# Attention scores in three passes over 128 rows with the remainder in four row groups, and transposes by single query tiles

## What is computed

```python
scores = jnp.einsum('bhqd,bhkd->bhqk', q, k) * scaling
scores = scores + attn_bias[:, None, :, :]
attn = jax.nn.softmax(scores, axis=-1)
ctx = jnp.einsum('bhij,bhjd->bhid', attn, v)
x = _rmsnorm(x + ctx @ wo + bo, alpha1, gamma1)
ff = jax.nn.silu(x @ w1 + b1) @ w2 + b2
x = _rmsnorm(x + ff, alpha2, gamma2)
```

## Time and profile before

| | us |
|---|---|
| median of three executions | 1954.26 |
| lowest, highest | 1952.67, 1956.72 |
| the profiled execution | 1954.66 |
| its span in the profile | 1952.9 |
| attention phase (to the first L1356) | about 1031.8 of the span |
| one batch (one `xT` load to the next) | 475.03 to 537.73 |

### The profile page before, as it was taken

One profiled execution on the slowest core, in us unless ns is written; L12 is line 12 of the kernel. 1 busy time (PEld: TensorE's weight loads), 2 busy tenths in 40 slices (PEclk: granted clock), 3 DMA queues, 4 the chain that ended last, 5 costly groups with the idle time before them and its releaser, 6 DMA issues. The chain is left out here.

```text
span 1952.9 us, 35623 instructions
## 1 busy us (share of the span) xinstructions
PE 1923.0 (98%) x10336; PEld 1694.0 (87%) x10336; DVE 1326.7 (68%) x2315; ACT 1169.7 (60%) x1893; POOL 691.6 (35%) x806
## 2 busy tenths in 40 slices
PE   7999999999999999999999999999999999999998
PEld 5888888888888888888887999999999999999997
DVE  5777777777777777777887566566666655656654
ACT  4777777777877778777875444344444334444432
POOL 2000000000000000000246657666666766666653
PEclk9999999999999999999999999999999999999999
DMA  7555665556555665557744221122222112222001
GB/s 211 155 143 153 167 158 135 138 155 184 132 143 147 163 168 130 139 154 210 172 129 146 87 87 54 40 78 86 86 86 83 52 40 82 86 86 86 30 28 41
DMA packets 107796, 226.87 MB, mean 116 GB/s; under 512 B 15088, under 2 KB 43504, under 8 KB 105712
## 3 DMA queue, kind: packets, MB, share of 16 engines
q1 hardware_dynamic: 107760, 226.43, 40.2%
HBM read 108.93 MB, written 41.94 MB: 77 GB/s over the span
## 5 line engine op out<-in xcount | busy, mean ns | idle before, releaser
L772 DVE TENSOR_TENSOR pT_lo<-ps_t,pT_hi 128x1024 fp32r<-128x1024 f32 x256 | 313.4, 1224 | 139.7 <-ACT pT_hi L660 139.7
L660 ACT ACTIVATE pT_hi<-ps_t 128x1024 fp32r<-128x1024 f32 x256 | 262.7, 1026 | 179.6 <-PE ps_t L916 178.6
L562 POOL TENSOR_TENSOR in_lo<-rows,in_hi 128x512 fp32r<-128x512 f32 x48 | 63.7, 1329 | 858.8 <-ACT in_hi L639 858.8
L653 ACT ACTIVATE probs<-probs,neg_max 128x512 f32<-128x512 f32 x512 | 339.2, 713 | 2.4 <-DVE neg_max L764 2.3
L764 DVE CUSTOM_DVE_ANT_0 probs<-ps_s,adj_s 128x512 f32<-128x512 f32 x448 | 290.8, 687 | 40.9 <-PE ps_s L907 33.9
L1300 DVE TENSOR_TENSOR h_lo<-hidden,h_hi 128x512 fp32r<-128x512 f32 x192 | 168.8, 879 | 172.5 <-ACT h_hi L1237 172.4
L916 PEld LDWEIGHTS ps_t<-ident,probs 128*128 128x128 f32 x2048 | 239.9, 141 | 35.0 <-issue 0.4
L916 PE MATMUL ps_t<-ident,probs 128*128 128x128 f32 x2048 | 265.7, 272 | 0.2 <-DVE pT_lo L772 0.2
L1395 PE MATMUL ps_y<-w_hi,h_hi 128*128 128x384 f32 x768 | 257.9, 336 | 0.0
L1395 PE MATMUL ps_y<-w_hi,h_lo 128*128 128x384 f32 x768 | 256.8, 334 | 0.0
L1395 PE MATMUL ps_y<-w_lo,h_hi 128*128 128x384 f32 x768 | 256.8, 334 | 0.0
(11 more groups left out here) (111 smaller groups left out, 3749.9 us busy)
## 6 DMA issues: line engine op xcount, KB each, us to landing
q_both<-weights_lo SPq DMA_DIRECT2D x192, 192.0 KB, 3.9
ctx_dram<-ctx_stage SPq DMA_DIRECT2D x128, 224.0 KB
ctx_raw<-ctx_dram SPq DMA_DIRECT2D x16, 1792.0 KB, 7.2
k_hl<-weights_hi SPq DMA_DIRECT2D x192, 96.0 KB, 3.4
adj_first<-in_adj SPq DMA_DIRECT2D x32, 512.0 KB, 9.2
adj_s<-in_adj SPq DMA_DIRECT2D x32, 512.0 KB, 6.1
rows<-in_xT SPq DMA_DIRECT2D x16, 768.0 KB, 7.1
rows<-in_x SPq DMA_DIRECT2D x16, 768.0 KB, 6.1
```

The costliest lines, as they stand in the source:

```text
L653: nc.scalar.activation(probs[:, at, :], probs[:, at, :], ACT.Exp, scale=-1.0, bias=neg_max[:, at:at + 1]).then_inc(exp_done, 1)
L660: nc.scalar.activation(pT_hi[:, h % 2, 2 * pair:2 * pair + 2, :, :], ps_t[pair][:, :, :].rearrange("p q (k i) -> p q k i", k=TT), ACT.Copy)\
L772: nc.vector.tensor_tensor(pT_lo[:, h % 2, s, :, :].rearrange("p q k i -> p (q k i)"), ps_t[pair][:, :, :].rearrange("p q n -> p (q n)"), p ...
```

## The change

A head's scores now take three products, without low by low. The two operands `q_wide` and `k_wide` have 128 rows: q high, q high, the first 32 features of q low, against k high, k low, the first 32 features of k high. One matmul of 128 rows per query tile multiplies them. The last 16 features of q low by k high are a matmul of 16 rows; the four query tiles' ones lie at partitions 0, 32, 64 and 96 (four row groups of the array), each with its own copy of q's and k's rows. Group 1 is filled by a DMA (q) or is already there in `k_wide` (k); for the groups 0, 2 and 3 GpSimd makes six copies per head (`copy_tails`), of 16 x 512 for k and 16 x 128 for q, each behind a no-op, a k copy before the q copy of its group. The four score banks of a head are filled in one stretch at the even steps, one head ahead (`AHEAD` = 2): four matmuls of 128 rows, then the four of 16 rows. `ps_s` has four banks, `ps_t` two banks of one tile each. Transposes, pT_hi and pT_lo go by single tiles, and a tile's transposes wait for pT_lo of the tile before the last. The four logits of a head follow the two pT_lo of the even step on VectorE; v2 and v3 are ahead of the scores on TensorE. k2 moves from step 0 to 4, q0 from 6 to 7, the copies of x from steps 2, 3, 4 to 5, 5, 6, and the loads of the bias from 11 and 12 to 13. q's second high copy is gone. The stacking takes 11, 14 and 12 DMAs for the three tiles of q and 9, 11 and 9 for those of k, each of one part.

```diff
+TAIL = 32
+TAIL_ROWS = DH - TAIL
+GROUP = 32
+OWN = 1
+COPIED = (0, 2, 3)
+HIGH, LOW = 0, 1
+STACKS = {"q": [(HIGH, 0, 0, DH), (HIGH, DH, 0, DH), (LOW, 2 * DH, 0, TAIL), (LOW, None, TAIL, DH)],
+          "k": [(HIGH, 0, 0, DH), (LOW, DH, 0, DH), (HIGH, 2 * DH, 0, TAIL)]}
...
+def stacks_of(kind, t):
+    out = []
+    for h in heads_of_tile(t):
+        for part, row, first, past in STACKS[kind]:
+            for tile, src, dim, n in pieces_of_head(h, first, past):
+                if tile == t:
+                    out.append((h, part, None if row is None else row + dim - first, src, n))
+    return out
...
+def tail_heads(t):
+    return [h for h in range(H) if pieces_of_head(h, TAIL, DH)[0][0] == t]
...
-STACK_DMAS = [2 * len(heads_of_tile(t)) for t in range(KT)]
+STACK_DMAS = {kind: [len(stacks_of(kind, t)) for t in range(KT)] for kind in "qk"}
...
-AHEAD = 3
-SIDE = {0: ["k2"], 1: ["v0", "v1"], 2: ["v2", "v3"], 6: ["q0"], 8: ["k0"], 10: ["q1"], 12: ["k1"], 14: ["q2"]}
-XT_AT = (2, 3, 4)
+AHEAD = 2
+SIDE = {1: ["v0", "v1"], 2: ["v2", "v3"], 4: ["k2"], 7: ["q0"], 8: ["k0"], 10: ["q1"], 12: ["k1"], 14: ["q2"]}
+XT_AT = {5: (0, 1), 6: (2,)}
...
-PARTS_HI = {"q": (0, 2), "k": (0,)}
 WO_STEPS = ["q0", "k0", "q1", "k1"]
 W1_PARTS = 2
+W1_ORDER = (0, 3, 1, 2, 4, 5)
+W1_AT = {3: 2, 5: 3, 8: 4, 10: 5}
+SCALE_AT = {11: (0,), 13: (1,), 14: (2, 3)}
...
-        q_both = sb("q_both", [2 * DH, H, 2, N], FP32R)
-        k_hl = sb("k_hl", [2 * DH, H, N], FP32R)
+        wide_of = {"q": sb("q_wide", [WIDE, H, N], FP32R), "k": sb("k_wide", [WIDE, H, N], FP32R)}
+        tails = sb("tails", [P, H, N], FP32R)
+        q_tails = sb("q_tails", [P, H, P], FP32R)
...
-        ps_s = [pb(f"ps_s{i}", [P, N]) for i in range(2)]
-        ps_t = [pb(f"ps_t{i}", [P, 2, N]) for i in range(2)]
+        ps_s = [pb(f"ps_s{i}", [P, N]) for i in range(TT)]
+        ps_t = [pb(f"ps_t{i}", [P, N]) for i in range(2)]
...
+        x1T_banks = ps_s[0:KT]
...
-                sp.wait_ge(proj_hi, proj_hi_no(b, kind, t, len(PARTS_HI[kind])))
-                for h in heads_of_tile(t):
-                    for tile, src, dst, n in pieces_of_head(h):
-                        if tile != t:
-                            continue
-                        for part, row in enumerate((dst, DH + dst)):
-                            if kind == "q":
-                                to = q_both[row:row + n, h, :, :]
-                                part_of = stage[kind][src:src + n, part:part + 2, :]
-                            else:
-                                to, part_of = k_hl[row:row + n, h, :], stage[kind][src:src + n, part, :]
-                            sp.dma_start(to.bitcast(FP32), part_of.bitcast(FP32)).then_inc(stacked[kind][t], DMA)
+                sp.wait_ge(proj_hi, proj_no(b, kind, t))
+                for h, part, row, src, n in stacks_of(kind, t):
+                    to = tail(tails, OWN)[:, h, :] if row is None else wide_of[kind][row:row + n, h, :]
+                    sp.dma_start(to.bitcast(FP32), stage[kind][src:src + n, part, :].bitcast(FP32))\
+                        .then_inc(stacked[kind][t], DMA)
...
+                    for i in W1_ORDER[0:2]:
+                        load_w1(i)
+                if p in W1_AT:
+                    sp.wait_ge(w1_lo_done, W1_AT[p] - 1)
+                    load_w1(W1_ORDER[W1_AT[p]])
+                if p == 8:
...
-                    if p in (11, 12) and not last:
-                        load_adj_pair(b + 1, p - 11)
+                    if p == 13 and not last:
+                        load_adj_pair(b + 1, 0)
+                        load_adj_pair(b + 1, 1)
...
+            def copy_tails(b, h):
+                t = pieces_of_head(h, TAIL, DH)[0][0]
+                for kind in "qk":
+                    wait_apart(pool, stacked[kind][t], DMA * STACK_DMAS[kind][t] * (b + 1), consts_ready)
+                n = tails_no(b, h) - 2 * len(COPIED)
+                for g in COPIED:
+                    wait_past(pool, tails_copied, n)
+                    pool.nop(nofuse=True)
+                    pool.tensor_copy(tail(tails, g)[:, h, :], wide_of["k"][TAIL:DH, h, :]).then_inc(tails_copied, 1)
+                    pool.wait_ge(tails_copied, n + 1)
+                    pool.nop(nofuse=True)
+                    pool.tensor_copy(tail(q_tails, g)[:, h, :], tail(tails, OWN)[:, h, g * P:(g + 1) * P])\
+                        .then_inc(tails_copied, 1)
+                    n += 2
...
-                for p in XT_AT:
-                    xT_low(b + 1, p - XT_AT[0])
+                behind_tails(b, H - 1 - len(tail_heads(KT - 1)))
+                for ks in XT_AT.values():
+                    for k in ks:
+                        xT_low(b + 1, k)
+                pool.wait_ge(xT_split, KT * (b + 2))
+                for h in tail_heads(KT - 1):
+                    copy_tails(b, h)
+                for t in range(KT - 1):
+                    for h in tail_heads(t):
+                        copy_tails(b + 1, h)
...
+                pool.wait_ge(proj_ready, proj_no(LAST, "q", 2))
...
-                if kind == "q":
-                    act.wait_ge(proj_hi, proj_hi_no(b, kind, t, 1))
-                    nc.scalar.activation(stage[kind][:, 2, :], stage[kind][:, 0, :].bitcast(FP32), ACT.Copy)\
-                      .then_inc(proj_hi, 1)
...
-                wait_past(act, v_ready, TT * b)
+                wait_past(act, proj_ready, 2 * KT * b)
...
-            def pT_high(b, h, pair):
-                act.wait_ge(transposed, pair_no(b, h, pair))
+            def pT_high(b, h, qt):
+                act.wait_ge(transposed, score_no(b, h, qt))
                 wait_past(act, pv_ready, H * b + h - 1)
-                nc.scalar.activation(pT_hi[:, h % 2, 2 * pair:2 * pair + 2, :, :],
...
-                    pT_high(b, p // 2, p % 2)
-                    for of, h, pair in pairs_of(b, p + AHEAD):
-                        exponent(of, h, 2 * pair)
-                        exponent(of, h, 2 * pair + 1)
+                    h, pair = p // 2, p % 2
+                    pT_high(b, h, 2 * pair)
+                    pT_high(b, h, 2 * pair + 1)
+                    if pair == 0:
+                        values_high(b, p)
                     if last:
                         first_square(p)
...
+                    for of, ahead, half in pairs_of(b, p + AHEAD):
+                        exponent(of, ahead, 2 * half)
+                        exponent(of, ahead, 2 * half + 1)
+                    for of, done, _ in context_at(b, p):
+                        stage_context(of, done)
+                    if pair == 1:
+                        values_high(b, p)
+                    for step, kind, t in steps_of(p, b, ("q", "k")):
+                        project_hi(batch_of(step, b), kind, t, shared_bank(step))
+                    for k in XT_AT.get(p, ()):
...
                         else:
-                            project_hi(batch_of(step, b), kind, t, shared_bank(step))
...
+                            xT_high(b + 1, k)
...
-                    wait_apart(dve, transposed, pair_no(b, h, pair) - 4, consts_loaded)
...
+                    wait_apart(dve, transposed, score_no(b, h, qt) - 2 * TT, consts_loaded)
+                    nc.vector.tensor_tensor_reduce(out=probs[:, at, :], in0=ps_s[qt][:, :],
...
+            def pT_low(b, h, qt):
+                dve.wait_ge(pT_hi_done, score_no(b, h, qt))
+                nc.vector.tensor_tensor(pT_lo[:, h % 2, qt, :, :].rearrange("p k i -> p (k i)"), ps_t[qt % 2][:, :],
+                                        pT_hi[:, h % 2, qt, :, :].rearrange("p k i -> p (k i)").bitcast(FP32),
                                         ALU.subtract).then_inc(pT_lo_done, 1)
...
+                    h, pair = p // 2, p % 2
+                    pT_low(b, h, 2 * pair)
+                    pT_low(b, h, 2 * pair + 1)
                     for step, kind, t in steps_of(p - 1, b, "qk"):
                         project_lo(batch_of(step, b), kind, t, shared_bank(step))
                     if last:
                         first_norm(p)
-                    pT_low(b, p // 2, p % 2)
-                    if p in (6, 8, 10, 12) and isinstance(b, int) and b == LAST - 1:
-                        shared.invert_sums(dve, 0, (p - 6) // 2)
-                    if last:
                         seam(p)
                     for _, _, kt in steps_of(p, b, "v"):
                         v_lo(b, kt)
+                    if pair == 0:
+                        for of, ahead, _ in pairs_of(b, p + AHEAD):
+                            logits(of, ahead)
+                    if p in (6, 8, 10, 12) and isinstance(b, int) and b == LAST - 1:
+                        shared.invert_sums(dve, 0, (p - 6) // 2)
...
-            def scores(b, h, qt):
...
-                        pe.wait_ge(stacked["k"][t], DMA * STACK_DMAS[t] * (b + 1))
-                wait_past(pe, logits_ready, score_no(b, h, qt) - 2)
```

(63 more changed lines are left out.)

167 lines of the change are left out of this document (70 added, 97 removed).

## The result

The change makes the kernel slower: 2109.0 us (2108.4 to 2109.8, four executions) against 1953.5 us (1952.3 to 1956.7), a ratio of 1.079 (95% interval 1.0778 to 1.0804). The forecast had the sign and a third of the size: +58 us instead of +155.5, outside its range.

A forecast was written before the change was run, and what follows sets the result against it. TensorE's instruction stream bounds the kernel before; after, waits on a ScalarE-VectorE ring, copies and SyncE reach it. 15 batches x 3.4 = 51, + 6 start + 1 end = 58 on 1954.7: 2012 us, range of all 1968 to 2050.

The forecast's parts named there:

- TensorE's part: TensorE in attention: scores cost 1.37 instead of 1.84 us per head; its own work falls by 3.8 to 58.6 per batch.
- between them I take 0.45: Four 16-row matmuls per head on TensorE: 0.45 us, between 0.23 at once and 0.92 one after another.
- The two copiers: pT_hi on ScalarE and pT_lo on VectorE by single tiles: 0.49 and 0.60 us each, some 1 us per batch each.
- The ring: Even steps: ScalarE waits 1.58 us for VectorE's logits before the first exponential; 6.46 us per head, 7.05 with a projection.
- The head by head waits: Walk of four engines through a batch's eight heads: 65.7 us per batch, 58.6 of it work and 7.1 TensorE's waits.
- There SyncE is late: SyncE, steps 8 to 15: 57 DMAs, 36 us of issue with 32 at hand, so q2's high part waits.
- Start and end: Start: +6 us, from later stackings, then k1's DMAs and tail copies; last batch: +1 us.
- The bounds: Same walk with one price changed: from 64.0 us per batch (SyncE never limiting) to over 68.4 (0.81 per DMA).
- SyncE becomes the bound: Rival, SyncE's queue: at 0.70 us per DMA 68.4 us per batch, total 2055; chance 0.10.
- The signs that I had named: Profile: ScalarE idle 1.6 us at even steps, TensorE busy under 60, x and tail-copy waits, SyncE nearly gapless, starts 0.1 apart.

The follow-up runs named there:

- e9: The changed kernel with 96-row matmuls instead of 128-row ones and 48 stackings per batch instead of 66, leaving some products out: 2025.6 us, ratio 1.037.
- e15: e9 with ScalarE's exponentials made one pair ahead of the transposes instead of two: 1996.0 us, ratio 1.021.
- e10: e9 with exponentials one pair ahead and the side work (k2, q0, copies of x) at the places of the kernel before: 1983.3 us, ratio 1.015.
- e12: The kernel before with each pT_hi and pT_lo copy of 1024 columns cut into two of 512: 1951.6 us, ratio 0.9995.
- e1: The changed kernel with each head's context store issued from ScalarE's queue instead of SyncE's: 2066.0 us, ratio 1.057.

## Why the prediction was wrong

By its own steps:

- **TensorE's part: mis-sized.** "Its own work per batch falls to 58.6." Busy share times period gives 61.4 (`e9`), 61.5 (`e15`) and, with the clock's 1.5 in it, 62.9 (after). The term "between them I take 0.45" was right (0.44); what I priced at nothing are the changes: 1.10 instead of 1.01 ahead of it (0.92, and the 0.09 after transposes that my sum holds elsewhere), 0.33 instead of 0.23 behind it. A head without waits takes 7.24, not 7.06: 0.18 per head, 1.5 of the 2.8 us. At least part of the rest is no price but short waits that busy time hides, as in the transposes shown at `e10`; how much of it was not summed up. By the Trainium skill (TensorEngine Tiling, Key Properties) changing the mode drains the array; the trace agrees, at some 0.1 us per change. The Trainium skill's figure of 3.07 for four row tiles (TensorE: Matmul & The Clock Gate, Measured speedup vs the span model), given for tiles of 32 rows, is 2.5 here with 16 rows, 1.12 against 0.44, before the changes are paid.
- **The two copiers: right.** pT_hi 597 ns, pT_lo 686 ns, as the rows of 512 columns had it; `e12` shows no cost.
- **The ring: right in mechanism.** 1.53 us of standing (1.58 forecast), heads 5 and 6 at 7.24 (7.06). Worth 1.8 us alone, 2.4 with room on SyncE.
- **The head by head waits: the step that failed.** Measured from one first pT_hi to the next in the eight heads from 473.46 on (heads 1 to 7, then head 0 of the next batch): head 0 11.15 (9.5 forecast), 1 10.57 (8.7), 2 8.13 (7.26), 3 9.0 (10.0), 4 8.08 (8.7), 5 and 6 7.24 each (7.06), 7 9.07 (7.4). The excess is in heads 7, 0, 1 and 2. I wrote "There SyncE is late" of heads 5 to 7 alone and let only q2's high part wait: with 36 us of issue against 32 at hand, a backlog of 4 us was priced at 0.3. I counted the 57 DMAs and left out what is queued behind them, the context stores. The chain is stackings, store, `ctx_stage`, bank, v matmuls. `e1` gives 3.0 us for it, `e9` 5.0 for the stackings that cause it. The waits that I did price were there and smaller: heads 3 and 4 are under their forecasts, and head 5's scores, where I had 1.68, waited 0.63 for the tail copies.
- **The clock: left out.** I priced no fall, as before has none. It costs 1.2 to 1.5 us per period: 1.5 is 62.9 less 61.4, 1.2 is TensorE's busy time in each 5 us of this stretch times what its granted clock lacks to 1.00.
- **Start and end: mis-sized.** Up to the first of the two loads, +21.0, of which 8.4 are one ordinary batch: 12.6 instead of 6 (TensorE waits 7.0 for the first tail copies). The last batch, +15.4 instead of +1: TensorE waits 4.5 for tail copies behind w1 splits, 4.7 for a low part, 8.4 for pT_lo, and its clock from 1113 us on is 0.88.
- **The bounds** varied prices of instructions and DMAs, one at a time, on a walk with a wait missing: no such variation reaches 2109. The issue itself measured 0.62 to 0.63. The rival "SyncE becomes the bound" named the right engine for the wrong reason, longer issues.

The signs that I had named came in part: 1.53 us before the exponentials, the waits for x and tail copies, SyncE with hardly a gap from 503.79 to 545.3 (steps 8 to 15). TensorE's busy time was not under 60, and the four starts lay 0.01 us apart, not 0.1.

The sum of errors: 15 x 5.0 = 75 (8.4 instead of 3.4, where 65.7 less 62.4 would have been 3.3) + 6.6 + 14.4 = 96 of 97 us. That the 65.7 us of the forecast stand so near `e9` (65.93) is luck: there 61.4 busy and 4.6 of waits, not 58.6 and 7.1, and with 18 stackings fewer than the forecast was made for.

How the 155.5 us divide, in the order in which they were taken away: 18 stackings 83.4 (2109.0 to 2025.6), the exponentials 29.6, the places 12.7; 29.8 are left in `e10`. There the period is 63.26, of which TensorE is busy for 61.8, 0.7 less than before: 11 us in all, against +9.0 at the start and +11.9 at the end. By the heads without waits, 7.24 against 7.54, TensorE's own work is 2.4 us less per batch, some 36 in 15 batches (an estimate); no version here turned that into time, and none beats the kernel before. What was not tried: a stacking with fewer DMAs that computes everything and needs no GpSimd copies, and another order of the last batch.

## What to carry to other kernels

When a change adds DMAs to a queue, list everything that stands behind them in it and follow each item to the buffer that it frees; here the first transfer that hurt, the store, was none of those added. A queue can be full long before its time is: SyncE in the kernel after issues for some 51 of 70.9 us (66 stackings at 0.63, 8 stores at 0.86, 2.5 of loads), but in bursts with deadlines. In the kernel before, 20 more stackings cost 1.5 us a batch and 30 more 9.6. And when one limit is removed, measure the next one beside it: the same edit was worth 1.8 us or 2.4, two good edits together no more than the weaker one alone.
